# Groups of four orders in the first stage, order 256 first, the record fill and the last stage's weights moved, a reordered drain, and one-body loops

## The reference, cut to what matters

```python
# x (64, 256 l, 257 m, 2); sqrt_eig (256 l, 257 m); pct (257 m, 256 l, 256 lat)
coeff = complex(x[..., 0], x[..., 1]) * sqrt_eig
h = irfft(einsum('nlm,mlk->nkm', coeff, pct), n=512, norm='forward')   # (64, 256, 512)

xn = layernorm(h)                                                      # over the 512
logits = tanh(einsum('bsd,btd->bst', xn @ K, xn) + bias)
logits = (logits - 10000 * (1 - band)) * temperature                   # band of 12 around the diagonal
h = h + softmax(logits) @ xn

x2 = layernorm(h)
mask = (x2[..., 0] >= 0.5) & (x2[..., 1] >= 0.5)
# four 4-bit numbers (first place over 0.5 of 16) and one value of each row go through
# seven 160x160 layers with relu, for two of eight positions; the two results are rounded
# to 0..15, and 2.0 is added at one of 16 places each, where mask holds
h = h + ffn(x2)
```

## Time and profile before

| | us |
|---|---|
| median of 3 runs (1553.82 to 1558.54) | 1555.68 |
| profiled execution, its own time | 1560.17 |
| its span, first to last instruction | 1558.4 |
| stage 1, to the first load of stage 2 | 347.9 |
| stage 2, to the first instruction of stage 3 | 995.6 |
| stage 3 | 214.9 |

### The profile page before, as it was taken

How to read it: one execution, slowest core, us unless ns; L and a number is a source line. 1 busy time by engine, 2 the same in 40 slices (tenths; PEclk the granted TensorE clock), 3 DMA queues, 4 the chain that set the end, 5 groups by cost and what they waited for, 6 DMA issues and landing times. The chain is left out here.

```text
span 1558.4 us, 31615 instructions
## 1 busy us (share of the span) xinstructions
PE 1388.7 (89%) x9389; PEld 1218.4 (78%) x9389; DVE 1084.0 (70%) x2564; ACT 676.2 (43%) x1373; POOL 615.6 (40%) x1598
## 2 busy tenths in 40 slices
PE   4777778857999999999999999999999997399993
PEld 3656666647999999999999999999999996255551
DVE  1322222216899999999999999999999985377762
ACT  1222221212455554554554554545545543377762
POOL 2000000001465565566556655655655555203222
PEclk9799998988999999999999999999999998699997
DMA  9999999972221221122112212211222110100000
GB/s 371 428 429 429 428 429 428 428 254 82 70 70 70 69 82 69 69 74 77 69 68 82 68 67 77 73 67 69 78 71 68 55 44 29 36 2 13 9 3 5
DMA packets 58748, 210.58 MB, mean 135 GB/s; under 512 B 9413, under 2 KB 12177, under 8 KB 46289
## 3 DMA queue, kind: packets, MB, share of 16 engines
q1 hardware_dynamic: 47360, 172.29, 28.3%
q10 hardware_dynamic: 5200, 33.62, 5.4%
q0 software_dynamic: 6144, 4.14, 0.9%
HBM read 138.73 MB, written 73.07 MB: 136 GB/s over the span
## 5 line engine op out<-in xcount | busy, mean ns | idle before, releaser
L187 PE MATMUL s1b<-pg,cg 128*128 128x256 f32 x1024 | 249.6, 406 | 89.0 <-DVE cg L138 84.0
L187 PEld LDWEIGHTS s1b<-pg,cg 128*128 128x128 f32 x1024 | 206.7, 204 | 131.5 <-ACT stage L215 37.6
L426 PE MATMUL ps_kx<-xThi,Khi 128*128 128x256 f32 x1024 | 284.1, 277 | 4.0 <-DVE xTlo L678 4.0
L427 PE MATMUL ps_kx<-xTlo,Khi 128*128 128x256 f32 x1024 | 283.7, 277 | 0.0
L428 PE MATMUL ps_kx<-xThi,Klo 128*128 128x256 f32 x1024 | 283.7, 277 | 0.0
L138 DVE TENSOR_TENSOR cg<-xg,se 128x2048 f32<-128x2048 f32 x32 | 73.3, 2292 | 234.9 <-DMA pg<-in_pct_dram 227.5
L585 ACT ACTIVATE o<-h,sh,sc 128x512 f32<-128x512 f32 x128 | 97.5, 809 | 266.8 <-POOL sh L818 266.8
L426 PEld LDWEIGHTS ps_kx<-xThi,Khi 128*128 128x128 f32 x1024 | 193.6, 189 | 4.6 <-DVE xTlo L678 4.6
L427 PEld LDWEIGHTS ps_kx<-xTlo,Khi 128*128 128x128 f32 x1024 | 193.3, 189 | 0.0
L428 PEld LDWEIGHTS ps_kx<-xThi,Klo 128*128 128x128 f32 x1024 | 193.2, 189 | 0.0
L215 ACT COPY stage<-s1b 128x512 f32<-128x512 f32 x128 | 65.6, 599 | 235.5 <-PE s1b L187 235.5
(11 more groups left out here) (138 smaller groups left out, 3216.2 us busy)
## 6 DMA issues: line engine op xcount, KB each, us to landing
pg<-in_pct_dram SPq DMA_DIRECT2D x32, 2048.0 KB, 27.7
xg<-in_xs_dram SPq DMA_DIRECT2D x32, 1024.0 KB, 22.9
spec<-stage ACTq DMA_DIRECT2D x64, 512.0 KB, 8.5
xt<-spec SPq DMA_DIRECT2D x64, 512.0 KB
out_dram<-o SPq DMA_DIRECT2D x64, 512.0 KB, 2.8
recs<-rec POOLq DMA_DIRECT2D x16, 160.0 KB, 16.4
recs<-rec,idx POOLq DMA_INDIRECT x128
Kf<-in_K_dram SPq DMA_DIRECT2D x1, 1024.0 KB, 23.7
```

What stands on the lines that cost most here:

```text
L187: last = nc.tensor.matmul(bank[(b % 2) * 4 + m // 2][:, m % 2, :], cg[:, b % 2, m * 2 + h, :], pg[:, b, m * 2 + h, :], start=(h == 0), sto ...
L426: nc.tensor.matmul(out_ap, whi, mhi, start=(j == 0), stop=False)
L427: nc.tensor.matmul(out_ap, whi, mlo, start=False, stop=False)
```

## The change

Stage 1: `GM` is 4, there are 64 groups, eight buffers (`RING1 = 8`) of half the size, and four `cg` sets of half the size (`SETS = 4`), each with two PSUM banks. A load of `xg` is now 512 KB and one of `pg` 1 MB, in pieces of 4 and 8 KB per partition. PE signals after each pair of orders (`PARTS = 2` a group), ACT copies pair by pair and stores after every second group, so that a store has the size it had. Order 256 is loaded first, into its own tiles, and multiplied first, into bank 7; ACT copies its row over the row of order 0's imaginary part, which is kept nowhere, and it goes out with the first store. Its own last turn is gone. Of the constants, K and seven others are loaded there, after five groups.

The fill of `recs`, the load of the last stage's weights and of five other constants of that stage are issued by SP in stage 2, after the loads of images 0 to 3. POOL waits for the fill before its first slot. The weights' split is done by ACT and DVE at the start of stage 3.

```diff
-GM = 8
+GM = 4
-RING1 = 4
+RING1 = 8
+SETS = 4
+PARTS = GM // 2
@@ stage 1, sync
             sp.dma_start(se[:, :], se_in).then_inc(se_loaded, 16)
+            sp.dma_start(x_top[:, :, :], xs_in[:, GROUPS * GM * 2:, :]).then_inc(top_loaded, 16)
+            sp.dma_start(p_top[:, :, :], pct_in[:, GROUPS * GM * 2:, :]).then_inc(top_loaded, 16)
             for b in range(RING1):
                 load(b, b)
-                if b == 1:
-                    for dst, src in ((Kf[:, :, :], K_in), (Wf[:, :, :], Wm_in), (W1f[:, :, :], W1_in), *others):
+                if b == RING1 // 2:
+                    for dst, src in ((Kf[:, :, :], K_in), *others):
                         sp.dma_start(dst, src).then_inc(const_loaded, 16)
...
-            sp.wait_ge(summed, GROUPS - RING1 + 1)
-            sp.dma_start(xg[:, 0, 0:2], xs_in[:, GROUPS * GM * 2:, :]).then_inc(loaded[0], 16)
-            sp.dma_start(pg[:, 0, 0:2], pct_in[:, GROUPS * GM * 2:, :]).then_inc(loaded[0], 16)
@@ stage 1, tensor
+                for part in range(PARTS):
+                    for m in (2 * part, 2 * part + 1):
+                        for h in range(2):
+                            last = nc.tensor.matmul(bank[(b % SETS) * PARTS + part][:, m % 2, :],
+                                                    cg[:, b % SETS, m * 2 + h, :], pg[:, b, m * 2 + h, :],
+                                                    start=(h == 0), stop=(h == 1))
+                    last.then_inc(summed, 1)
@@ stage 1, gpsimd: removed
-            for q in range(NB * NLAT // (P * 8)):
-                pool.dma_start(view[:, q], rec0[:, :, :]).then_inc(rec_stored, 16)
@@ stage 2, sync
             for n in range(4):
                 load(n, n)
+            sp.wait_ge(const.rec_filled, 2)
+            empty = recs.rearrange("(p q r) w -> p q r w", p=P, r=8)
+            for q in range(NB * NLAT // (P * 8)):
+                sp.dma_start(empty[:, q], const.rec0[:, :, :]).then_inc(rec_emptied, 16)
+            for dst, src in ffn_consts:
+                sp.dma_start(dst, src).then_inc(ffn_loaded, 16)
@@ stage 2, gpsimd
             def slot(i, k, has):
+                draining = isinstance(i, int) and i > NB
...
+                if has(i - 2) and draining:
+                    output_factors(i - 2, k % 2)
                 if has(i - 3):
                     ...                                   # the record of image i-3
-                if has(i - 2):
-                    ...                                   # the same factors
+                if has(i - 2) and not draining:
+                    output_factors(i - 2, k % 2)

             pool.wait_ge(consts_set, 5)
             pool.wait_ge(dcT_set, 1)
+            pool.wait_ge(rec_emptied, 16 * (NB * NLAT // (P * 8)))
             slots(nc.gpsimd, slot)
@@ stage 3
-        def steps(eng, ahead, body):
+        def steps(eng, at_once, ahead, body, phases=1):
             count = eng.value_load(const.count_i[0:1, 0:1], min_val=0, max_val=NB * NLAT)
+            at_once()
             with eng.If(count > 0):
                 ahead()
-            with eng.Fori(0, STEPS, 2) as s0:
-                for u in range(2):
+            with eng.Fori(0, STEPS, phases) as s0:
+                for u in range(phases):
@@ stage 3, sync
-            sp.wait_ge(start, 2)
-            steps(nc.sync, lambda: load(0, 0), body)
+            load(0, 0)
+            steps(nc.sync, lambda: None, lambda: sp.nop(), body, phases=2)
@@ stage 3, vector
-            nc.vector.memset(rt[:, :, :, :], 0.0).then_inc(rec_used, 1)
+            dve.wait_ge(weight_hi, 2)
+            ...                                   # W1r, Wlo, W1r scaled, W1: the four operations of split_weights
+            steps(nc.vector, lambda: features(0, 0), first, body, phases=2)
@@ stage 3, scalar
+            nc.scalar.copy(W1h[:, :, :], const.W1f[:, :, :]).then_inc(weight_hi, 1)
+            nc.scalar.copy(Whi[:, :, :], const.Wf[:, :, :]).then_inc(weight_hi, 1)
+            steps(nc.scalar, lambda: round_in(0), first, body)
@@ stage 3, tensor
+            pe.wait_ge(weight_lo, 4)
+            steps(nc.tensor, lambda: features_T(0), first, body)
```

More of the change, by code:

```diff
@@ L196, in _ @@
                     multiply(g0 + b, b)
-            pe.wait_ge(scaled, GROUPS + 1)
-            pe.wait_ge(copied, (GROUPS - 1) * 4)
-            for h in range(2):
-                last = nc.tensor.matmul(bank[0][:, 0, :], cg[:, 0, h, :], pg[:, 0, h, :],
-                                        start=(h == 0), stop=(h == 1))
-            last.then_inc(summed, 1)
         @block.scalar
@@ L206, in copy_out @@
             def copy_out(g, b):
-                act.wait_ge(summed, g + 1)
-                if isinstance(g, int):
-                    wait(act, stored[b % 2], 32 * (g // 2))
-                else:
-                    act.wait_ge(stored[b % 2], g * 16 - 16 * (b % 2))
-                if isinstance(g, int) and g == 0:
-                    nc.scalar.copy(const.dc[:, :], bank[0][0:NB, 0, :])
-                for j in range(4):
-                    nc.scalar.copy(stage[:, b % 2, 2 * j:2 * j + 2, :],
-                                   bank[(b % 2) * 4 + j][:, :, :]).then_inc(copied, 1)
@@ L217, in copy_out @@
-                act.wait_ge(copied, g * 4 + 4)
-                for c in range(2):
-                    act.dma_start(spec[:, bass.ds(g * GM + c * NLAT, GM), :],
-                                  stage[c * NB:(c + 1) * NB, b % 2]).then_inc(stored[b % 2], 16)
+                half, at = (b // 2) % 2, (b % 2) * GM
+                act.wait_ge(summed, g * PARTS + 1)
+                if b % 2 == 0:
+                    if isinstance(g, int):
+                        wait(act, stored[half], 32 * (g // 4))
+                    else:
+                        act.wait_ge(stored[half], g * 8 - 16 * half)
@@ new lines, in copy_out @@
+                for j in range(PARTS):
+                    if j > 0:
+                        act.wait_ge(summed, g * PARTS + j + 1)
+                    if isinstance(g, int) and g == 0 and j == 0:
+                        nc.scalar.copy(const.dc[:, :], bank[0][0:NB, 0, :])
+                    nc.scalar.copy(stage[:, half, at + 2 * j:at + 2 * j + 2, :],
+                                   bank[(b % SETS) * PARTS + j][:, :, :]).then_inc(copied, 1)
+                    if isinstance(g, int) and g == 0 and j == 0:
+                        act.wait_ge(copied, 1)
+                        act.wait_ge(top_summed, 1)
+                        nc.scalar.copy(stage[0:NB, 0, 0, :], bank[7][0:NB, 1, :]).then_inc(top_kept, 1)
+                        act.wait_ge(top_kept, 1)
@@ L222, in _ @@
+                if b % 2 == 1:
+                    act.wait_ge(copied, g * PARTS + PARTS)
+                    for c in range(2):
+                        act.dma_start(spec[:, bass.ds(g * GM + (c * NLAT - GM), 2 * GM), :],
+                                      stage[c * NB:(c + 1) * NB, half]).then_inc(stored[half], 16)
             for b in range(RING1):
                 copy_out(b, b)
-                if b == 0:
-                    act.wait_ge(const_loaded, 16 * (3 + len(others)))
-                    for hi, full in ((const.Khi, Kf), (const.Whi, Wf), (W1h, W1f)):
-                        nc.scalar.copy(hi[:, :, :], full[:, :, :]).then_inc(const_hi, 1)
+                if b == RING1 // 2:
+                    act.wait_ge(const_loaded, 16 * (1 + len(others)))
+                    nc.scalar.copy(const.Khi[:, :, :], Kf[:, :, :]).then_inc(const_hi, 1)
@@ L230, in _, with stage2_blocks @@
                     copy_out(g0 + b, b)
[L231 to L249 removed]
+            for half in range(2):
+                act.wait_ge(stored[half], 32 * (GROUPS // 4))
+def stage2_blocks(nc, const, ffn_consts, spec, recs, out):
     with ExitStack() as ctx:
@@ L1038, in body @@
                     relu(s + 1, 1)
-            steps(nc.scalar, first, body)
+            nc.scalar.copy(W1h[:, :, :], const.W1f[:, :, :]).then_inc(weight_hi, 1)
+            nc.scalar.copy(Whi[:, :, :], const.Wf[:, :, :]).then_inc(weight_hi, 1)
+            steps(nc.scalar, lambda: round_in(0), first, body)
         @block.tensor
@@ L1140, in body @@
                 results_T(s)
-            steps(nc.tensor, first, body)
+            pe.wait_ge(weight_lo, 4)
+            steps(nc.tensor, lambda: features_T(0), first, body)
         @block.gpsimd
@@ L1159, in _ @@
             nc.gpsimd.memset(oc[:, :, :], 0.0).then_inc(oc_free, 1)
-            steps(nc.gpsimd, lambda: pool.nop(), body)
+            steps(nc.gpsimd, lambda: None, lambda: pool.nop(), body)
 def build(nc, xs, pct, se, K, temp, bias, W1, Wm, W5, W7, fb, dft, band, w16, row, tri, ident, sel, iota, out):
```

156 lines of the change are left out of this document (77 added, 79 removed).

## The result

| | before | after |
|---|---|---|
| median, us (7 runs each) | 1555.68 (1553.82 to 1558.54) | 1562.04 (1561.20 to 1564.33) |
| profiled execution, own time | 1560.17 | 1564.04 |
| its span | 1558.4 | 1562.2 |
| SP's first load of stage 2 | 347.9 | 342.5 |

The changed kernel is slower: ratio 1.0045, 95% interval 1.0036 to 1.0055. Beside it on one chip later, the medians were 1562.81 and 1554.69, ratio 1.0046 (1.0029 to 1.0063). The forecast was 1551.6, with a range of 1544 to 1560.

What follows compares the result with a forecast made beforehand. Stage 1 was taken as bound by DMA engines, stage 2 by PE except at its ends, stage 3 by a chain following PE. Terms -11.2 + 3.0 + 3.5 + 1.2 - 1.9 + 1.3 gave -4.1: 1551.6 us, range 1544 to 1560.

Steps and rivals of the forecast that it cites:

- last loads land: End of stage 1: fewer bytes, more packets, smaller early gap and stores that catch up; last load at 324.4 us, -4.6.
- chain behind them: End of stage 1: scale, products, copies and store after the last load take 12.3 us instead of 18.9, -6.6.
- start of stage 2: Start of stage 2: POOL waits for the fill, there 15.1 us after SP's first issue instead of 12.1, +3.0.
- drain: End of stage 2: POOL idles ahead of image 63's factors and begins its last record later, +3.5 (3.3 to 4.1).
- steps: Stage 3: one loop body may end the hole and long steps (-4.1) or not (0), taken as -1.9.
- The packets: Stage 1: halved pieces of xg and pg add packets and completions at 7.5 ns each, 4.3 us more.
- The early gap: Stage 1, 28 to 34 us: DMA engines not full; fewer constants and more queued loads win back half, -1.0.
- stores further ahead: Stage 1: with groups of half the size more stores are done when the last load lands, +1.2.
- rival C: Start of stage 2: fill lands as slowly as in stage 1, costing 14.3 instead of 3.0; 1562.9 us, chance 0.07.
- B: Stage 1: only its end gets shorter, -6.6 instead of -11.2; 1556.2 us, chance 0.18.
- A: Stages 1 and 3: finer loads cost nothing and the hole goes, -10.6; 1545.1 us, chance 0.14.
- D: Stage 1: the rate falls to the 398 GB/s of 2 KB packets, +15; about 1571 us, chance 0.04.

Runs made afterwards that it cites:

- The loads in pairs: The changed kernel with the loads of two neighbouring groups in one transfer, except the last two groups: 1557.09 us, ratio 1.0011 to the kernel before.
- The moved wait: The changed kernel with POOL's wait for the fill moved from its first slot to right ahead of its first indirect store: 1557.30 us, ratio 1.0012.
- One early transfer: The changed kernel with one of the 16 fill transfers issued by POOL in stage 1, the other 15 by SP in stage 2: 1559.43 us, ratio 1.0023.
- The kernels with four edits: The changed kernel with old drain order, POOL's wait moved, one fill transfer in stage 1, paired loads: 0.9947, 0.9963; with all fill in stage 1: 0.9994.

## Why the prediction was wrong

The forecast went by a sum of steps. The table sets each against what was found, in us. The start of stage 2 is a difference of medians, the others come from profiles.

| step | forecast | found |
|---|---|---|
| last loads land | -4.6 | -0.1 |
| chain behind them | -6.6 | -6.3 |
| start of stage 2 | +3.0 | +4.7 |
| POOL's first transfer | not seen | +3.5 |
| drain | +3.5 | +4.0 |
| start of stage 3 | +1.2 | +0.9 |
| steps | -1.9 | 0 |
| end | +1.3 | +0.6 |
| sum | -4.1 | +7.3 |

The medians differ by 6.4, on one chip by 8.1. Two steps failed above all: the landing of the last loads, put at -4.6 and found at -0.1, and POOL's first transfer, which no term had and which cost 3.5.

*The loads.* Here the forecast failed most. In seven profiles with the changed stage 1 the last scale starts at 326.6 to 329.9 us, mean 328.6; in five with the old one at 328.2 to 329.3, mean 328.7. That bytes cost time there is shown (without the fill's 2.46 MB stage 2 began 4.2 us sooner), their full price of 9.1 us is not. The packets were sized right: 422 instead of 428 GB/s over 280 us are 4.0 us against a forecast 4.3. The loads in pairs gave it back: in four profiles with them the last scale starts at 322.5 to 325.2 us, mean 323.8. Two other terms went wrong. The early gap did get smaller (349 GB/s instead of 297), but taken over the first 40 us the rate fell from 373 to 366 GB/s, 0.28 MB, +0.7 us instead of -1.0. And the last loads do not run at the full rate: 276 instead of 369 GB/s from 320 to 330 us, 0.9 MB or 2.2 us. I had divided bytes by the rate of the middle up to the last byte. Some 2 us are left. For 1.2 of them stores further ahead were forecast; a term that was missing fits the other part. Order 256's own load, 0.39 MB or 0.9 us at 428 GB/s, stood behind the last `pg` and now stands ahead of all groups. The bytes moved up to the last landing are in line with it: 138.5 MB (421 GB/s up to 328.98 us) before and 135.1 MB (411 GB/s up to 328.78) after, 3.4 MB less and not 3.9. How the 2 us divide is an estimate. That the store of 1 MB between the last loads holds them is argued from the windows; no run took it away.

*The chain* was right: 12.6 us in five of seven profiles, 13.7 and 13.8 in two, forecast 12.3; with the old stage 1 18.9 us in three of five, 20.6 and 22.0 in two. The table has 12.6 against 18.9; by the means it would be -7.0. In the profile after, the clock of PE was at half from 325.9 to 329.3 us, which is where its extra microsecond lies.

*The fill* was the right mechanism with too small a price. In seven profiles POOL starts 16.2 to 18.0 us after SP, forecast 15.1, before 12.1. I had counted the time on the DMA engines, 7.3 us; SP alone needs 11.3 us to issue the sixteen. The moved wait brought 4.7 us. POOL's start stayed below the 19.2 us that rival C needed. C's time of 1562.9 is the nearest of all to the measured 1562.04, but by luck: its cause, a start 26.4 us after SP, did not come.

*POOL's first transfer* is a cost that the forecast did not have at all. It did not decide the sign by itself: without it the kernel is still at 1.0023. In the kernel before POOL's first transfers are the fill in stage 1, where nobody waits for POOL. I moved them to SP's queue and did not ask what POOL's next one would be. It is the first indirect store, which then costs 2.3 us more ahead and 0.5 in length. Of the 3.5 us that this costs, 2.5 come through ACT's wait for `sh`; the other 1.0 falls where PE is idle for 2.1 us and at half clock for 3.4. One early transfer took all of it away. Why the first transfer is slow, the profile doesn't show.

*The drain* was right: 4.0 us, forecast 3.5 with bounds of 3.3 to 4.1.

*The steps.* The long ones of the earlier trace rows go with the chip or the moment, and not with one body or two on PE, ACT and POOL: three kernels, each run word for word the same on two chips, had them on one and not on the other. In all, seven profiles on two chips have them, and none of eight on the third, taken in two sessions; for the very first pair of profiles the chip is not on record. I had given half of 4.1 us for a cause the trace did not name. The long profiles also differ in SP's loop. At the line of its `If`, one comparison or register operation takes 0.7 to 1.4 us in seven of the eight long profiles, and the shortest 2 to 5 ns in all eight; in the nine others each takes 34 to 50 ns.

The Trainium skill, page "Runtime: NRT & Kernel Launch", section "Instruction fetch mechanics", has the rule that a taken branch out of the fetched window stalls its engine. The forecast had drawn from it that the hole would vanish with a smaller loop. The kernels with four edits have the smaller loop on PE, ACT and POOL, and long steps. But SP and DVE kept two bodies in every run, and the pauses of 2.3 us are on DVE. So the runs refute the forecast's use of the rule and leave the rule itself untested; the cause stays open.

*Numbers across chips.* The profile before came from an execution with long steps (own time 1560.17 against a median of 1555.68, and above the slowest of the seven runs, 1558.54), the one after from one without. So the -1.9 was priced on steps that the median did not need to have. The difference of the two spans, 3.8 us, hides 3.4 us of steps; this is why the table says 0 for a chip without long steps.

On the rivals: B was nearest on stage 1 (only the end gets shorter) and too low by 6 us since it had neither the first transfer nor the full price of the wait. A's free packets were refuted, D's rate of 398 GB/s too.

## What to carry to other kernels

When a transfer moves from one queue to another, look at what becomes the first transfer of the queue it leaves, and who waits for it. A wait for a bulk of small transfers costs at least the time to issue them; place it ahead of the first instruction that touches their data. A stage that is full of bytes is full only in its middle: price the last loads and the first from their own windows. Profile on a second chip before a hole that no engine released is given a price; a second profile alone, on a chip with long steps, showed long steps again.

## What was not expected of the hardware

- The first transfer that POOL issues in a program started 2.9 to 3.3 us after the instruction ahead of it when it was an indirect store in stage 2 (seven profiles), and 0.6 us after it when another had gone before.
- On one chip all steps of stage 3 were 35.2 us, on two others the same programs had some steps of 35.9 to 41.6, in four of seven profiles with a pause of 2.3 us on DVE that no engine released. Their medians are 0.4% apart for the kernel before.
- A turn of POOL's loop without work takes 0.43 us in one kernel and 0.63 in another with the same instructions in the loop and other code ahead of it: 2 us at the end of the program.
- Halving pieces of 16 KB and 8 KB per partition costs 1.4% of the rate (422 instead of 428 GB/s), and the rate comes back with the old pieces.
